# An attention and mixture-of-experts layer on one core: query stacks moved in 4 KB pieces, expert weights in four transfers from ScalarE's queue

## The reference, cut to what matters

```python
def reference(x, w_qkv, w_out, b_out, gate_w, gate_b, w1, b1, w2, b2, wg, bg, w3, b3):
    x = _layernorm(x + attention(x, w_qkv, w_out, b_out))     # window of 64 keys
    return _layernorm(x + moe(x, gate_w, gate_b, w1, b1, w2, b2, wg, bg, w3, b3))

# attention, for each of 16 heads
scores = q @ k.T / sqrt(8)           # -inf unless j <= i and i - j < 64
ctx = softmax(scores) @ v            # then ctx @ w_out.T + b_out

# moe: top 2 of 8 logits, softmax over the two
x1 = x @ w1[e] + b1[e];  x2 = x @ w2[e] + b2[e]
s = silu((x1 * x2) @ wg[e] + bg[e])
y = s @ w3[e] + b3[e]                # out += weight_of_e * y
```

## Time and profile before

| | |
|---|---|
| median of 3 runs | 309.66 us (307.4 to 311.45) |
| the profiled execution, its own time | 311.95 us |
| its span, first to last instruction | 310.2 us |
| mean granted TensorE clock | 0.939 of full speed |
| attention with routing, about | 0 to 152 us |
| expert tiles, about | 152 to 286 us |
| end, about | 286 to 310 us |
| busy: TensorE, VectorE, GpSimd, ScalarE | 237.9, 217.2, 161.0, 154.1 us |

### The profile page before, as it was taken

How to read it: one execution, slowest core, us unless ns; L and a number is a source line. 1 busy time by engine, 2 the same in 40 slices (tenths; PEclk the granted TensorE clock), 3 DMA queues, 4 the chain that set the end, 5 groups by cost and what they waited for, 6 DMA issues and landing times.

```text
span 310.2 us, 7675 instructions
## 1 busy us (share of the span) xinstructions
PE 237.9 (77%) x1791; PEld 174.1 (56%) x1791; DVE 217.2 (70%) x714; ACT 154.1 (50%) x410; POOL 161.0 (52%) x287
## 2 busy tenths in 40 slices
PE   2386579898979998887597878699999999995000
PEld 1155367676757777775355555566766766764000
DVE  6499537888878988886646677677777776774091
ACT  3636537868676968645125633244444334332043
POOL 6654002667666777777643662223464654656151
PEclk9999979999999999999679999999999999999555
DMA  4563425459686979766320112211111111100522
GB/s 119 181 157 91 137 75 143 128 149 273 195 249 189 281 203 268 181 202 240 113 60 3 36 53 68 78 37 51 42 56 32 51 40 45 48 18 7 201 104 101
DMA packets 33988, 36.50 MB, mean 118 GB/s; under 512 B 4972, under 2 KB 30062, under 8 KB 33824
## 3 DMA queue, kind: packets, MB, share of 16 engines
q1 hardware_dynamic: 30864, 29.69, 33.5%
q0 software_dynamic: 2336, 4.37, 4.3%
q10 hardware_dynamic: 752, 2.03, 2.0%
HBM read 25.48 MB, written 11.05 MB: 118 GB/s over the span
## 4 chain that ended last, share of the span: by engine, by line
PE 47%; DVE 14%; SPq 12%; issue 12%; DMA 8%; POOL 3%; ACT 2%; DVEq 0%; ACTq 0%; POOLq 0%
PE bank L1578 9%; PE bank L1550 8%; PE bank L1541 6%; SPq L409 5%; PE bank L1393 3%; DMA k_stack<-k_scratch 3%; PE bank L1573 2%; PE bank L1397 2%; PE bank L1566 2%; PE bank L1412 2%; DMA expert_out<-probs,tile_x 2%; DVE top L954 2%; SPq L422 2%; DVE shift L964 2%; DMA w_up<-expert_out 2%
## 5 line engine op out<-in xcount | busy, mean ns | idle before, releaser
L713 POOL DMA_INDIRECT expert_out<-probs,tile_x x39 | 40.3, 1034 | 58.2 <-DVE probs L1272 56.2
L813 ACT ACTIVATE probs<-bank 128x512 f32<-128x512 f32 x64 | 34.8, 592 | 20.0 <-PE bank L1397 19.6
L664 POOL DMA_INDIRECT routed<-rows,place x32 | 33.2, 1037 | 21.4 <-issue 16.5
L1578 PE MATMUL bank<-w_up,x_unit 128*128 x78 | 41.7, 617 | 0.0
L1550 PE MATMUL bank<-w_gate,x_all 128*128 x156 | 40.4, 382 | 0.5 <-DVE v_aug L1263 0.5
L1277 DVE TENSOR_TENSOR w_rows<-bank,b_up 128x512 f32<-128x512 f32 x39 | 26.8, 688 | 18.5 <-PE bank L1578 18.3
L964 DVE TENSOR_TENSOR shift<-top,delta_block 64x256 fp32r<-64x256 f32 x64 | 30.1, 471 | 11.9 <-PE bank L1397 9.5
L1541 PEld LDWEIGHTS bank<-w_down,xT 128*128 128x128 f32 x156 | 20.4, 190 | 31.2 <-issue 31.2
L888 ACT COPY x_unit<-bank 128x128 f32<-128x128 f32 x39 | 10.3, 264 | 55.3 <-PE bank L1558 55.1
L1393 PE MATMUL bank<-q_stack,k_stack 128*128 128x256 f32 x128 | 28.4, 305 | 10.9 <-issue 7.4
L954 DVE TENSOR_REDUCE top<-bank 128x4 f32<-128x384 f32 x64 | 33.5, 549 | 2.0 <-PE bank L1376 1.3
(11 more groups left out here) (177 smaller groups left out, 538.2 us busy)
## 6 DMA issues: line engine op xcount, KB each, us to landing
k_stack<-k_scratch SPq DMA_DIRECT2D x28, 160.0 KB, 3.2
q_stack<-q_scratch SPq DMA_DIRECT2D x62, 64.0 KB, 2.5
tile_x<-routed SPq DMA_DIRECT2D x39, 65.0 KB, 1.8
k_scratch<-k_parts SPq DMA_DIRECT2D x7, 320.0 KB
q_scratch<-q_parts SPq DMA_DIRECT2D x8, 256.0 KB
w_up<-in_L_ffn_w_dram SPq DMA_DIRECT2D x16, 128.0 KB
w_gate<-in_L_ffn_wg_dram SPq DMA_DIRECT2D x8, 256.0 KB
b_up<-in_L_ffn_b_dram SPq DMA_DIRECT2D x2, 1024.0 KB
```

Of the source, the lines that this page charges most:

```text
L664: eng.indirect_dma_start(routed, bass.IndirectOffsetOnAxis(ap=place[i][:, k:k + 1], axis=0), rows[i][:, k, :], None, bounds_check=SPARE + ...
L713: eng.indirect_dma_start(expert_out, bass.IndirectOffsetOnAxis(ap=tile_x[i][:, P:P + 1].bitcast(I32), axis=0), y[i][:, :], None, bounds_ch ...
L813: eng.activation(probs[t[1] % 2][a][:, 512 * h:512 * h + 512], t_bank[h][:, :], ACT.Exp).then_inc(probs_ready, 1)
L1578: eng.matmul(up_bank[:, :], tile_xT[n[1] % 2][:, :], of_expert(w_up, e[0])).then_inc(up_made, 1)
```

## The change

- `stack_queries` keeps its eight transfers and their 64 KB, but `q_stack` is stored with the group index inside (partition, h, g, n in place of partition, g, h, n), so that a partition gets one run of 1024 numbers where it got four of 256. `shifted_scores` reads the new order. In the code `stack_keys` is written with a merged last dimension too.
- The 32 weight transfers of SyncE's loop go. ScalarE issues w1 and w2 whole (1 MB each) after its work of slot 2, wg (2 MB) and w3 (1 MB) at the end of slot 3. The counts on `experts_loaded` follow.
- GpSimd clears `q_stack[1]` right behind its two stack transfers, before it waits for them. The bias is added in four pieces, behind a wait for `k_lo` of unit 1; the residual waits for all four.

```diff
         def stack_queries(eng, i, part):
...
-                q_stack[i][64 * dup + hh:64 * dup + hh + 61:4, :, hh, :].bitcast(F32),
-                q_scratch[i].rearrange("w (d h g) n -> h (w d) g n", d=HD, h=4)[hh])
+                q_stack[i][64 * dup + hh:64 * dup + hh + 61:4, hh, :, :].rearrange("p g n -> p (g n)").bitcast(F32),
+                q_scratch[i].rearrange("w (d h g) n -> h (w d) (g n)", d=HD, h=4)[hh])
...
-            return eng.dma_start(k_stack[i][32 * part:32 * part + 32, :, :].bitcast(F32),
-                                 k_scratch[i][part // 2].rearrange("(r g) n -> r g n", g=4))
+            return eng.dma_start(k_stack[i][32 * part:32 * part + 32, :, :].rearrange("p g n -> p (g n)").bitcast(F32),
+                                 k_scratch[i][part // 2].rearrange("(r g) n -> r (g n)", g=4))
...
-                if s is None:
-
-                    e = t[0] * 4 + (t[1] - 4)
-                    for c, w in enumerate((w1, w2)):
-                        eng.dma_start(w_up[:, bass.ds(e, 1), c, :],
-                                      w[bass.ds(e, 1)].rearrange("e h f -> h e f")).then_inc(experts_loaded, 16)
-                    for held, w in ((w_gate, wg), (w_down, w3)):
-                        eng.dma_start(held[:, bass.ds(e, 1), :, :].rearrange("p e c n -> p (e c) n"),
-                                      w[bass.ds(e, 1)].rearrange("e (c p) n -> p (e c) n", p=P)).then_inc(experts_loaded, 16)
...
-                if s == -1:
-
-                    eng.memset(q_stack[1][:, :, :, :].bitcast(F32), 0.0).then_inc(zeros_ready[1], 1)
                 if s == 1:
 
                     eng.wait_ge(loaded, 16 * 4)
-                    eng.tensor_tensor(x_all[:, :, :], x_all[:, :, :], bo[:, :].unsqueeze(1).to_broadcast([P, STEPS, P]),
-                                      ALU.add).then_inc(xb_ready, 1)
+                    eng.wait_ge(k_lo, 2)
+                    for q in range(4):
+                        held = x_all[:, 4 * q:4 * q + 4, :]
+                        eng.tensor_tensor(held, held, bo[:, :].unsqueeze(1).to_broadcast([P, 4, P]), ALU.add).then_inc(xb_ready, 1)
...
+                    eng.memset(q_stack[1][:, :, :, :].bitcast(F32), 0.0).then_inc(zeros_ready[1], 1)
                     eng.wait_ge(first_stacked, 16 * POOL_PARTS)
...
+                if s == 2:
+                    for c, w in enumerate((w1, w2)):
+                        eng.dma_start(w_up[:, :, c, :], w.rearrange("e h f -> h e f")).then_inc(experts_loaded, 16)
                 if has(s, 3, STEPS + 2):
                     gap_of_two(later(t, -3))
+                if s == 3:
+                    for held, w in ((w_gate, wg), (w_down, w3)):
+                        eng.dma_start(held[:, :, :, :].rearrange("p e c n -> p (e c) n"),
+                                      w.rearrange("e (c p) n -> p (e c) n", p=P)).then_inc(experts_loaded, 16)
...
-                    eng.wait_ge(xb_ready, 1)
+                    eng.wait_ge(xb_ready, 4)
...
-                                   q_stack[i][:, grp, :, QT * w:QT * w + QT], start=(l == 0), stop=False,
+                                   q_stack[i][:, :, grp, QT * w:QT * w + QT], start=(l == 0), stop=False,
```

More of the change, by code:

```diff
@@ L401, in pcount @@
             return g * per + (c // 2 + 1) * per
+        Q_PARTS, K_PARTS = 8, 4
         POOL_PARTS = 2
+        STACKED = 16 * (Q_PARTS + K_PARTS)
         EARLY_LINKS, LATE_LINKS = 18, 14
@@ L452, in slot @@
                     i = u[1] % 2
-                    wait_apart(eng, wait_value, const_ready, stacked[i], pcount(later(u, -2), 192))
+                    wait_apart(eng, wait_value, const_ready, stacked[i], pcount(later(u, -2), STACKED))
                     wait(eng, q_hi, ucount(u, 1, 1))
@@ L473, in slot @@
                     eng.wait_ge(q_out, ucount(u, 16, 16))
-                    for part in range(8):
-                        if s != -2 or part < 8 - POOL_PARTS:
+                    for part in range(Q_PARTS):
+                        if s != -2 or part < Q_PARTS - POOL_PARTS:
                             stack_queries(eng, i, part).then_inc(stacked[i], 16)
@@ L478, in slot @@
                         eng.wait_ge(k_out, ucount(u, 16, 16))
-                        for part in range(4):
+                        for part in range(K_PARTS):
                             stack_keys(eng, i, part).then_inc(stacked[i], 16)
@@ L683, in slot @@
                     eng.wait_ge(zeros_ready[0], 1)
-                    for part in range(8 - POOL_PARTS, 8):
+                    for part in range(Q_PARTS - POOL_PARTS, Q_PARTS):
                         stack_queries(eng, 0, part).then_inc(first_stacked, 16)
+                    eng.memset(q_stack[1][:, :, :, :].bitcast(F32), 0.0).then_inc(zeros_ready[1], 1)
                     eng.wait_ge(first_stacked, 16 * POOL_PARTS)
@@ L735, in _ @@
             eng.wait_ge(early_chain, EARLY_LINKS)
-            eng.wait_ge(experts_loaded, 16 * (4 * E + 4))
+            eng.wait_ge(experts_loaded, 16 * (4 + 4))
             run_end(piece, tile_slot)
@@ L1386, in shifted_scores @@
                 wait(eng, shift_ready, count(t, 4, 2 * a + 2))
-                wait(eng, stacked[i], pcount(u, 192))
+                wait(eng, stacked[i], pcount(u, STACKED))
                 for h in range(2):
```

## The result

| | before | after |
|---|---|---|
| median | 310.56 us (4 runs, 307.4 to 312.75) | 316.77 us (4 runs, 316.22 to 322.66) |
| ratio after/before | | 1.022, 95% interval 1.016 to 1.029 |
| the profiled execution, its own time | 311.95 us | 316.54 us |
| its span | 310.2 us | 314.8 us |
| mean granted TensorE clock | 0.939 | 0.929 |

The ratio is that of the executions in the chip's usual state: one of the four before and one of the four after (322.66 us) ran in a slower one and are left out of it. The forecast was 305.6 us, with a range up to 311.0. The head of the page after, and its granted clock, to be held against the earlier trace rows: the sixth slice shows 8 tenths (7 before), and a new fall has come at the eighth and ninth (55 to 71 us), which showed 9 tenths before and 7 and 8 now.

The account below looks back on a forecast made before the run. It took TensorE's waits for the stacks in units 1 to 5 (10.36 us) as the bound. Units 1 to 5 gave -4.0, +0.6, +0.6, -0.7 and -0.6, together -4.1: 305.6 us from a median of 309.66, range 300.0 to 311.0.

Parts of the forecast that it names:

- The same weights as traffic: Weights on another queue delay the stacks' landing: 1.4 us in units 2 and 3, 0.7 in unit 4.
- Rival B: Weights hold the stacks up before steps 4, 6 and 8, 4.1 us each: 314.4 us, chance 0.10.
- Turns favour the stacks: On the DMA engines, a 5 KB stack piece takes far longer than a 1 KB weight piece; argued against rival B.
- The clock behind the stop: TensorE's clock after the stop before step 2: a shorter stop may spare its fall, 1.1 us, in rival A only.
- rival A: All goes well in units 1 to 5, the loop falls below the compute: -10.6 us, 299.1 us, chance 0.30.
- Memset moved ahead of the wait: GpSimd's 3.52 us memset, run earlier before unit 1, costs nothing, at most a few tenths.
- Bias addition behind k_lo: In unit 1 the low keys can start at about 24.53 in place of 27.71, 3.2 us earlier.
- Query issues: SyncE's eight query issues per unit take about 0.5 us each in place of 0.595: 0.8 us gained per unit.
- Unit 1: Its sum: -3.2 from the bias addition and -0.8 from the query issues, -4.0 us.
- Weights off SyncE's queue: In unit 4 the key store no longer waits behind queued weights and a load: 0.6 us gained, once.
- Weights on ScalarE's queue: Four issues, some 2.5 us of ScalarE's program in a stretch with slack; counted as nothing.
- rival C: ScalarE's full queue blocks wg or w3's issue at slot 3's end, about 6 us: 311.6 us, chance 0.08.

Follow-up runs that it names:

- e2: The changed kernel with the weights back in SyncE's loop: 0.987 of the kernel before, 310.48 us.
- e4: The kernel before with only the weights moved to ScalarE's queue: 1.020 of the kernel before, 320.2 us.
- e7: e3 with only w1 and w2 (2 MB) on ScalarE's queue in slot 2: 1.016 of the kernel before, 314.44 us.
- e13: e3 with w1 and w2 (2 MB) on SyncE's own queue, behind unit 2's stacks: 1.003 of the kernel before, 312.15 us.
- e8: e3 with the weights on ScalarE's queue expert by expert, 640 KB at each slot's end: 1.002 of the kernel before, 311.0 us.
- e14: e7 with its 2 MB cut into 16 transfers of 128 KB: 1.016 of the kernel before, 316.78 us.
- e1: The changed kernel with the memset back behind the landing of the first stacks: 1.009 of the kernel before, 315.73 us.
- e9: The kernel before with only the bias addition moved behind k_lo, in four pieces: 0.988 of the kernel before, 307.71 us.
- e6: e3 with each query transfer on 16 neighbouring partitions, so the attention is of other pairs: 303.47 us in one run.
- e15: e3 with five of eight query transfers issued before the wait for the low keys, the load of x behind them: 0.978 of the kernel before, 305.42 us.
- e12: e3 with five query transfers issued before the low keys' wait and the weights as in e8: 0.992 of the kernel before, 309.55 us.
- e16: e12 with x loaded as in e15, ScalarE issuing one expert's weights at even slots' start, one at odd slots' end: 0.999, 310.69 us.
- e3: The changed kernel with the weights back in SyncE's loop and the memset at its old place: 0.982 of the kernel before, 309.41 us.

## Why the prediction was wrong, step by step

- **"The same weights as traffic"** is the step that failed. It was sized at +1.4 us for units 2 and 3, between 0 and 4.1. Measured at unit 2: landing 9.65 us and not 3.47, +6.18, above my upper end. That end came from single scatters beside loads of other queues. A stack is twelve transfers in a chain with a store ahead, and the queue beside it held 2 MB already issued. A row of light company could not bound it. The experiments show the cause: with the part taken away the stop falls to 0.59 us (e2), the part alone has it (6.29, e4), 2 MB of it have it (6.56, e7), the same 2 MB on SyncE's own queue don't (e13), and doses of 640 KB don't (e8).
- **Rival B** had the place and the mechanism right, and the shape wrong. It put 4.1 us on each of three units. In truth unit 2 pays 6.2, unit 3 pays about 2 through the clock, and unit 4 nothing: its last key transfer takes 4.24 us to land, 4.62 before. The weights were through by then.
- **Turns.** "Turns favour the stacks" was wrong for the first 2 us: 99.4% against 0.0%, and the same in e7 (648 packets to none). The rule that I held against it, the Trainium skill, DMA: Bandwidth & Descriptors, Queues, rings and completion order, says that an engine serves queues in turns and drains a whole packet of descriptors, typically 9 to 17 and at most 64, before it changes. The rows from 52 us on (54.4% against 52.1%) agree with turns. Those from 48 to 50 don't fit the typical packet, but they don't refute the rule: by an estimate from the rows, 636 pieces on 16 engines are 40 for each, below the page's ceiling of 64. Likewise a weight transfer of 1 MB makes 64 pieces of 1 KB for each engine, and one of 128 KB, as in e14, makes 8, and there the queues shared from the start. What the page calls a packet the profile doesn't mark, so what holds SyncE's queue stays open.
- **The clock behind the stop** had no term for a stop that becomes longer. I counted a gain in rival A only. Unit 3 is later by 2.00 us, with 6 us at 0.57 of full speed behind the stop; e7 has the same 41 matmuls in 6 us at 0.58 with the DMA engines almost idle.
- **Memset moved ahead of the wait** is the second step that failed: "this costs nothing". I looked at what waits for GpSimd's signal and at L964, and not at what VectorE does from 15.7 to 19.2. It copies shift_w (L942), 3.38 us in place of 0.42, and that takes 2.0 of the 3.2 us at the low keys (e1). The Trainium skill, SBUF — State Buffer, Who interferes with whom, has two rules here and I used one: that a VectorE instruction with two SBUF inputs is held only by GpSimd's reads, with which L964 agrees (0.87 us beside the memset in the earlier trace rows); the other says that a copy or cast which runs in a mode with both port pairs contends with GpSimd, and that whichever of the two is issued first keeps the shared pair for its whole instruction. L942 agrees with the second: it starts behind a memset (15.69 to 19.23) that only writes, and ends at 19.52, 0.29 us after it.
- **Bias addition behind k_lo** was right: 24.56 in e1 and 24.20 in e9 against 24.53. The pieces cost L964 about 2.3 us in step 1, within my 2.5, and the stop hid them.
- **Query issues** were taken as 0.5 us, between 0.417 and 0.595. Measured 0.589: the upper end. The partition step sets it (e6: 0.420). The nearest row in shape was the key transfer, and it was without the step; I named that and still took the middle. So the 0.8 us per unit fall away as a term.
- **Unit 1** then reads: -3.2 for the bias addition, +2.0 for the memset, so about -1.2 at the low keys (27.71 to 26.59); the start of the unit moved by 2.34. The way from low keys to stack matmul takes 12.90 us before and 11.68 after. Most of that 1.22 us is single long issues: the eight query issues take 6.20 us there before, one of them 1.79, and 5.53 after; the four key issues 2.33 and 1.97. It isn't the new order: e9, which has the old one, takes 5.33 and 1.98. So about 1 us of the -2.34 comes from long issues that happened to lie there in the trace of before. That part is luck.
- **Weights off SyncE's queue** was right in unit 4: the store is issued at 80.63, 0.08 us after the low keys end at 80.55, where it was 0.68. But the query issues took 5.56 us there for 5.18, so the right sum (-0.67 for -0.7) is partly luck.
- **Weights on ScalarE's queue** was counted at nothing for its issues. One took 7.58 us, so rival C's mechanism came as it stood, in one of the two transfers it named (w3). The number of pieces isn't what made it long: wg, issued just ahead, has 2048 as well and took 0.37 us. It cost nothing that can be seen here because TensorE's stop lay over it. A standing ScalarE does cost once the stacks don't make the stop, as e14 shows, where the number of issues makes it and not a block.

## What to carry to other kernels

In this kernel bulk that was issued on a second queue did not wait behind a chain of small transfers on the first: 2 MB in two transfers got ahead, and TensorE paid twice, in the stop and in the clock behind it. Issue such bulk in small doses behind the small transfers on their own queue; the fastest kernel here that computes the same (e15) does that with 640 KB per slot. In one piece of 2 MB it only moves the stop to the next unit (e13), and doses on the other queue gave no long stop but no gain either (e8, e12, e16). Before a memset or any GpSimd instruction is moved, look at what VectorE copies in the new place, not only at who waits for GpSimd; and where issues bound a loop, look at the partition step of the transfer before its piece size.

## What the runs showed of the hardware that I had not expected

- A transfer whose 16 partitions are four apart took 0.589 us to issue, the same on neighbouring partitions 0.420 us, with equal bytes and runs (e3, e6).
- With 2 MB already given to ScalarE's queue in two transfers, SyncE's queue moved 1 packet in 2 us, and the other 636 (none and 648 in e7); with the same bytes in 16 transfers it was 87 and 404 (e14).
- The issue of w3 (1 MB in 2048 pieces), with 4 MB issued ahead of it on the same queue (part of them already moved), blocked ScalarE for 7.58 us; wg, with 2048 pieces too and 2 MB ahead of it, took 0.37 us. 14 issues of 128 KB took 9.03 us by their number (e14, median 0.454), where two of 1 MB had taken 1.27 us.
- A GpSimd memset, which reads nothing, held a fp32 copy of VectorE (0.42 us) for 3.38 us.
